# Another order for the beginning of a two-layer cross-attention kernel: the first queries ahead of the keys, the loads regrouped

## The chip, the cores and the metric

The kernel runs on one core of one Trainium2 chip. The metric is the device time of one execution in microseconds. TensorE (PE) multiplies and transposes, VectorE (DVE), ScalarE (ACT) and GpSimd (POOL) work beside it, and SyncE (SP) issues DMAs. ScalarE issues a few as well. Each of the two issues onto a queue of its own, and the two queues share the core's 16 DMA engines.

## The reference

Two cross-attention layers run one after the other over x (16 batches, 256 rows, 160 channels), with a context of 64 tokens by 256 channels for each batch. There are 20 heads of 8 channels.

```python
# layer 0
q = heads(x @ W_q); k_t, v_t = heads(text @ W_k), heads(text @ W_v)     # text = first 60 tokens
probs_t = softmax(q k_t^T * 8**-0.5); text_out = probs_t v_t
k_ip, v_ip = heads(ip @ W_k_ip), heads(ip @ W_v_ip)                     # ip = last 4 tokens
sem = l2norm(probs_t @ text) . l2norm(ip)
probs_ip = softmax(q k_ip^T * 8**-0.5 + 0.5 * sem) * spatial_mask
x = (text_out + probs_ip v_ip) @ W_out + b_out + x
# layer 1: HEADS = 20, TEXT_LEN = 77, so all 64 tokens are text
x = softmax(q k^T * 8**-0.5) v @ Wo.T + bo + x
```

## The kernel before, in words

Work goes by batch: g = 0 to 15 is layer 0, g = 16 to 31 is layer 1. A step t does the core of the attention for batch g = t and the preparation of later batches (t+1: scores for the row maxima; t+3, t+4: queries and keys), and the end of earlier ones (t-1, t-2). Tables written by hand set the order of every engine: `PE_STEP`, `ACT_STEP`, `DVE_STEP`, `POOL_STEP` and `SP_STEP` hold one list for each phase of steps (`PHASES`), and an entry `("q", 3, 0)` in step t means stage q of batch t+3. Stages of batches that do not exist are left out, and those in `ONCE` exist for batch 0 only. Semaphores carry all dependences, so an engine that waits holds everything behind it in its list.

What the beginning does:

- **Warm-up and first loads.** PE does four matmuls on zeros (L521). SP issues the first loads (L428 to L441), ScalarE the two halves of the context `ca` (L725).
- **Keys of layer 0**: PE `project_keys(0, n)` and `project_prompts` (all recorded as L500) for n = 0, later in stage `setup` for n = 1. ACT copies them to `kt` (L731, L738), DVE masks them (L395, L399).
- **Queries of batches 0 and 1** (stage q, for both batches' rows at once, one half of the channels each): PE L500 `ps<-x,wq`.
- **Splits.** Queries and keys are split into three bf16 parts: high (ACT L769, L778), remainder (DVE L845, L409), middle (ACT L773, L782), low (DVE L418, L413). SP then stacks copies of the parts into `qs` and `ks`, six DMAs each (L483 for queries, 160 KB each; L475 for keys, 80 KB each). The score matmuls (stage sc, L572) read only the stacks.
- **Keys of layer 1** (stage `keys1`): PE projects them from `ca` and `wk[1]`. It waits for `rest_in`, a semaphore that counts several loads. ACT copies them to `kt[1]`.
- **The first scores**: sc of batch 0 (L572), whose maxima DVE takes (L889, L898, L901), PE transposes (stage mt, L582), ACT copies (L805) and SP stacks (L488). Then st (L597) makes the scores for the exponentials, exp (L789) and u (L607) follow.
- **Stage vk** multiplies the context by the value weights (L500 `ps<-cw`). It reads `cw`, loaded at L461 (context) and L438 (weights).
- **The rest of x** (batches 4 to 15, 1920 KB) is loaded by SP at L452, the last of the loads that stage `late` holds.

PE order between the warm-up and the main steps, before: keys 0, queries 0 and 1, `setup`, `keys1`, sc of batch 0.

Of the kernel before, what the change touches and what calls it, by code (L numbers as in the profile page):

```python
# [31 lines left out]
N_IP = 4  # L32
# [15 lines left out]
KE = 2  # L48
# [66 lines left out]
def fixed(eng, v):  # L115
# [7 lines left out]

PHASES = (-1, 0, B, B + 2, N_G)
PE_STEP = [
# [14 lines left out]
ACT_STEP = [  # L140
    [("qh", 3, 0), ("kh", 3, 0), ("qm", 3, 0), ("setup", 2, 0), ("km", 3, 0), ("iplen", 2, 0), ("keys1", 2, 0)],
    [("kh", 3, 0), ("km", 3, 0), ("qh", 3, 0), ("mtev", 1, 0), ("qm", 3, 0), ("qh", 4, 0), ("qm", 4, 0)],
    [("exp", 0, 0), ("exp", 0, 1), ("ipe", -2, 0), ("exp", 0, 2), ("exp", 0, 3), ("exp", 0, 4), ("ztev", -2, 0),
# [81 lines left out]
def xattn_kernel(nc, xT, ctxT, ctx0, ctx1, side, WQ, WK, WKIP, WV, WVIP, WO0, WREM, WOP, WO1, BO,  # L225
# [3 lines left out]
    with ExitStack() as stack:  # L229
# [196 lines left out]
        def _(sp):  # L426

            sp.dma_start(wk[0][:, :, :], WK[0]).then_inc(c_in[0], 16)  # L428
            sp.dma_start(wkip[:, :, :], WKIP).then_inc(kv_in[0], 16)
            sp.dma_start(x[:, :, 0:2 * S], xT[:, :, 0:2 * S]).then_inc(x_in[0], 16)  # L430
            sp.dma_start(wq[0][:, :, :], WQ[0]).then_inc(w_in, 16)
            sp.dma_start(cst[:, :], consts).then_inc(w_in, 16)
            sp.dma_start(wvip[:, :, :], WVIP).then_inc(kv_in[1], 16)
            for n in range(2):
                sp.dma_start(ks[n][KR:KM].rearrange("r s a b t -> r (s a b) t"),
                             ones_rows[n].unsqueeze(1).broadcast_to([4, 4 * PAIRS, 128])).then_inc(rows_in, 16)
            for n in range(2):
                sp.dma_start(cw[:, n, :, M2[0] + T:], WV[0]).then_inc(rest_in, 16)  # L438
            sp.dma_start(id16[:, :], ident16).then_inc(rest_in, 16)
            sp.dma_start(x[:, :, 2 * S:4 * S], xT[:, :, 2 * S:4 * S]).then_inc(x_in[1], 16)  # L440
            sp.dma_start(wk[1][:, :, :], WK[1]).then_inc(rest_in, 16)  # L441

            def load_late(a, _):
# [41 lines left out]
            def stack_maxima(a, _):  # L485
# [10 lines left out]
        def _(pe):  # L496
# [25 lines left out]

            pe.wait_ge(c_in[0], 32)
            project_keys(0, 0)
            pe.wait_ge(c_in[1], 16)
            pe.wait_ge(kv_in[0], 16)
            project_prompts(wkip, 6)

            def setup(a, _):
# [9 lines left out]
            def keys1(a, _):  # L539

                pe.wait_ge(setup_sb, 8)
                pe.wait_ge(rest_in, 16 * 4)
                for n in range(2):
                    project_keys(1, n)

            def q(a, _):
                half, lay = a.base % 2, a.layer
                if lay == 0:
                    if a.base == 0:
                        pe.wait_ge(w_in, 32)  # L550
                        pe.wait_ge(x_in[0], 16)
# [164 lines left out]
            run(PE_STEP, {"q": q, "sc": sc, "mt": mt_, "st": st, "u": u, "pv": pv, "quad": quad, "vk": vk, "vw": vw,  # L716
                          "ot": ot, "zt": zt_, "y": y, "setup": setup, "keys1": keys1}, settle)(pe)


        @block.scalar  # L720
        def _(act):
            nc.scalar.preload_act_table_set("natural_log_exp_and_others")
            for n in range(2):
                cols = slice(n * 8 * T, (n + 1) * 8 * T)
                act.dma_start(ca[:, :, cols], ctxT[:, :, cols]).then_inc(c_in[n], 16)  # L725

            def keep_keys(layer, n, first):
# [6 lines left out]

            keep_keys(0, 0, 1)
            act.wait_ge(setup_ps, 4)
            for half in range(2):
                nc.scalar.copy(kt[0][:, half, :, T - N_IP:],  # L738
                               ps[0:HC, 6, half * 64:(half + 1) * 64].rearrange("p (b t) -> p b t", t=N_IP)).then_inc(setup_sb, 1)

# [66 lines left out]
            def ztev(a, _):  # L807
# [9 lines left out]
            run(ACT_STEP, {"otev": otev, "qh": qh, "qm": qm, "kh": kh, "km": km, "exp": exp, "rsq": rsq, "ipe": ipe,  # L817
                           "mtev": mtev, "ztev": ztev, "setup": setup, "iplen": iplen, "keys1": keys1})(act)


        @block.vector
        def _(dve):
# [4 lines left out]
            nc.vector.memset(vpb[:, :, :, 0:IP_ROW], 0.0).then_inc(zeroed, 1)  # L827
            dve.wait_ge(c_in[0], 32)
            dve.wait_ge(c_in[1], 16)
            ipc = ca[:, :, :].rearrange("p k (b t) -> p k b t", t=T)[:, :, :, T - N_IP:]  # L830
            for e in range(KE):
                last = nc.vector.tensor_tensor(ipsq[:, e, :].rearrange("p (b t) -> p b t", t=N_IP), ipc[:, e], ipc[:, e], ALU.mult)
            last.then_inc(sq_made, 1)
            dve.wait_ge(w_in, 32)
            dve.wait_ge(zeroed, 3)
            for n, col in ((0, C_MHH0), (1, C_MHH1)):
                for ring in range(2):
                    nc.vector.tensor_copy(vb[n][:, ring, :, SUM0:SUM0 + 2],
                                          cst[0:M2[n], col:col + 2].unsqueeze(1).broadcast_to([M2[n], PAIRS, 2])).then_inc(vsum, 1)

# [119 lines left out]
            def ysb(a, _):  # L960
# [3 lines left out]
                for mh in range(2):  # L964
# [145 lines left out]
```

## Time and profile before

| what | value |
|---|---|
| median of 3 runs | 513.9 us (513.51 to 517.48) |
| span of the profiled execution | 513.8 us, on core 0, the only one |
| PE busy | 473.6 us, 92% |
| DVE / ACT / POOL busy | 312.9 / 213.8 / 161.8 us |
| mean granted TensorE clock | 0.938 of full |

The profiled execution's own time beside its span: the runs listed are 513.9, 517.48 and 513.51 us, and the span of 513.8 us lies 0.1 us under their median, so the sum of the prediction is made against a span that stands for the median. A digit of the row PEclk is the TensorE clock in a fortieth of the span, in tenths of full speed. A row of the timeline is a run of like instructions of one engine. PE makes two passes for each of the kernel's float32 matmuls, so that `x8` in a row is four matmuls of the program.

### The profile page before, as it was taken

Reading aid. Unit: us, or ns where it says so; the run is one execution under the profiler, and the core shown is the slowest. Engines: PE = TensorE matmul, PEld = TensorE weight load, DVE = VectorE, ACT = ScalarE, POOL = GpSimd, SP = SyncE. Lnnn points to the kernel's source line nnn. Section 1 sums busy time; section 2 is a strip of 40 time slices with the busy share of each in tenths; the row PEclk is TensorE's granted clock in tenths of the full one; section 3 lists DMA queues with packets and bytes.
Section 4 is the critical chain, followed back from the end, with each engine's and each line's share of the span. In section 5 each row is a group of like instructions: output and inputs, shape, how many; then the busy total and the mean of one; then the engine's idle time right before and its main releaser. Section 6 shows DMA issues by size and latency. Waiting matters only on the chain.

```text
span 513.8 us, 10047 instructions
## 1 busy us (share of the span) xinstructions
PE 473.6 (92%) x3100; PEld 255.1 (50%) x3100; DVE 312.9 (61%) x1002; ACT 213.8 (42%) x463; POOL 161.8 (32%) x331
## 2 busy tenths in 40 slices
PE   8968889989999999999999996989898989897996
PEld 4333345545555455554554554555364545454553
DVE  2443686768877787777976776556364445455442
ACT  2413243344444434434354354445354444444361
POOL 0200252453445533555436453422212021221000
PEclk9986998999999999999999999899898597989699
DMA  8995709036073180640905409092728090919011
GB/s 199 130 202 110 95 4 131 18 52 82 18 97 53 31 102 16 83 64 12 120 18 75 64 4 122 8 137 54 115 53 113 23 138 26 139 39 153 2 28 40
DMA packets 33197, 38.15 MB, mean 74 GB/s; under 512 B 4984, under 2 KB 24488, under 8 KB 33000
## 3 DMA queue, kind: packets, MB, share of 16 engines
q1 hardware_dynamic: 32616, 36.63, 47.5%
q10 hardware_dynamic: 544, 1.05, 0.7%
q8 instruction: 20, 0.33, 0.3%
q14 instruction: 17, 0.14, 0.1%
HBM read 10.80 MB, written 2.62 MB: 26 GB/s over the span
## 4 chain that ended last, share of the span: by engine, by line
PE 70%; DMA 16%; SPq 5%; ACT 4%; issue 3%; DVE 1%; ACTq 0%; DVEq 0%
PE ps L500 23%; PE ps L607 14%; DMA qs<-qp 9%; PE ps L634 8%; PE ps L597 8%; PE ps L572 7%; DMA qs<-mt 6%; PE ps L681 4%; SPq L483 4%; PE ps L693 3%; PE ps L649 2%; ACT mt L805 1%; PE ps L582 1%; DMA ca<-in_ctxT 1%; SPq L488 1%
## 5 line engine op out<-in xcount | busy, mean ns | idle before, releaser
L789 ACT ACTIVATE pt<-ps 120x512 f32<-120x512 f32 (+1 forms) x160 | 90.3, 595 | 106.1 <-PE ps L597 105.5
L889 DVE TENSOR_REDUCE mx<-ps 128x8 f32<-128x480 f32 (+3 forms) x192 | 106.3, 577 | 11.6 <-PE ps L572 11.6
L607 PE MATMUL ps<-pt,gram 120*120 120x512 f32 x160 | 81.4, 606 | 0.7 <-ACT pt L789 0.7
L418 POOL TENSOR_TENSOR qp<-qr,qp 80x512 bf16<-80x512 f32 x28 | 32.2, 1151 | 151.9 <-ACT qp L773 151.9
L965 DVE SCALAR_TENSOR_TENSOR x<-ps,bo,x 80x256 f32<-80x256 f32 (+1 forms) x64 | 27.9, 476 | 72.3 <-PE ps L500 72.3
L597 PE MATMUL ps<-qs,ks 100*120 100x256 bf16 (+1 forms) x320 | 63.2, 294 | 8.3 <-DMA qs<-mt 6.0
L500 PE MATMUL ps<-x,wq 80*80 80x512 f32 (+1 forms) x128 | 66.4, 645 | 1.0 <-ACT mt L805 0.9
L572 PEld LDWEIGHTS ps<-ks,qs 96*128 96x128 bf16 x640 | 43.6, 103 | 45.1 <-issue 26.1
L572 PE MATMUL ps<-ks,qs 96*128 96x128 bf16 x640 | 56.9, 231 | 9.2 <-DMA qs<-qp 4.9
L634 PE MATMUL ps<-pt,vb 120*32 120x256 f32 (+1 forms) x640 | 64.3, 410 | 0.0
L500 PE MATMUL ps<-zt,wo 80*80 80x256 f32 (+1 forms) x192 | 55.2, 413 | 8.7 <-ACT zt L815 8.3
L853 DVE TENSOR_TENSOR wt<-ps,pt 120x512 f32<-120x512 f32 x80 | 55.1, 688 | 7.2 <-PE ps L607 3.8
L769 ACT CAST qp<-ps 80x512 bf16<-80x512 f32 x32 | 18.6, 581 | 84.2 <-PE ps L500 59.0
L597 PEld LDWEIGHTS ps<-qs,ks 100*120 100x120 bf16 (+1 forms) x320 | 30.9, 121 | 32.4 <-DMA qs<-mt 13.1
L500 PEld LDWEIGHTS ps<-zt,wo 80*80 80x80 f32 (+1 forms) x192 | 28.5, 159 | 27.5 <-DVE qr L845 9.8
L845 DVE TENSOR_TENSOR qr<-ps,qp 80x512 f32<-80x512 f32 x32 | 21.9, 684 | 29.6 <-ACT qp L769 29.5
L681 PE MATMUL ps<-cst,ots 128*128 128x128 f32 (+1 forms) x192 | 36.7, 286 | 0.8 <-ACT ots L763 0.8
L634 PEld LDWEIGHTS ps<-pt,vb 120*32 120x32 f32 (+1 forms) x640 | 16.5, 111 | 41.9 <-issue 38.4
L761 ACT COPY ots<-ps 128x512 f32<-128x512 f32 x32 | 18.6, 582 | 42.0 <-PE ps L634 41.9
L681 PEld LDWEIGHTS ps<-cst,ots 128*128 128x128 f32 (+1 forms) x192 | 26.0, 148 | 16.9 <-issue 13.0
L864 DVE RECIPROCAL rs<-ps 128x20 f32<-128x20 f32 x64 | 17.7, 277 | 26.4 <-PE ps L681 26.3
L607 PEld LDWEIGHTS ps<-pt,gram 120*120 120x120 f32 x160 | 24.7, 184 | 15.9 <-issue 11.8
(99 smaller groups left out, 605.6 us busy)
## 6 DMA issues: line engine op xcount, KB each, us to landing
qs<-qp SPq DMA_DIRECT2D x96, 160.0 KB, 5.5
ks<-kp SPq DMA_DIRECT2D x96, 80.0 KB, 6.4
cw<-in_ctx SPq DMA_DIRECT2D x16, 184.0 KB, 4.1
out_T<-x SPq DMA_DIRECT2D x16, 160.0 KB, 2.7
cw<-in_ctx SPq DMA_DIRECT2D x16, 128.0 KB, 3.8
x<-in_xT SPq DMA_DIRECT2D x1, 1920.0 KB, 15.2
ca<-in_ctxT ACTq DMA_DIRECT2D x2, 512.0 KB, 7.3
x<-in_xT SPq DMA_DIRECT2D x2, 320.0 KB, 8.9
```

The source lines that it names most:

```text
L418: tt(qp[:, 2, half, :], qr[:, :], qp[:, 1, half, :], ALU.subtract).then_inc(q_l, 1)
L500: last = nc.tensor.matmul(out, l, r, start=(n == 0), stop=(n == len(pairs_) - 1), **kw)
L572: last = nc.tensor.matmul(ps[:, bank, n * 128:(n + 1) * 128], qs[0:KR, slot, pair, c:c + 128], ks[a.layer][0:KR, slot, pair, b2, :], start ...
L597: last = nc.tensor.matmul(ps[0:m, 2 + (a.base + c) % 2, n * S:(n + 1) * S], ks[a.layer][0:KM, slot, pair, b2, 0:m], qs[0:KM, slot, pair, b ...
L607: nc.tensor.matmul(ps[0:M2[0], 4 + (a.base + c) % 2, :], gram[:, a.base % 2, :], pt[0:M2[0], a.base % 2, 2 * c:2 * c + 2, :].rearrange("p ...
L634: last = nc.tensor.matmul(out_of(pair), vb[a.layer][:, a.base % 2, pair, :], pt[0:m, a.base % 2, pair, :], start=(grp != 1), stop=(a.layer ...
L681: last = nc.tensor.transpose(ps[:, bank, grp * 128:grp * 128 + p], ots[0:p, grp, tile * 128:(tile + 1) * 128], cst[0:p, C_ID:C_ID + p])
L789: nc.scalar.activation(pt[0:m, a.base % 2, 2 * c:2 * c + 2, :].rearrange("p a b -> p (a b)"), ps[0:m, 2 + (a.base + c) % 2, :], ACT.Exp, s ...
L845: nc.vector.tensor_tensor(qr[:, :], ps[0:HC, bank_of("q", a, 0), :], qp[:, 0, half, :], ALU.subtract).then_inc(q_r, 1)
L853: nc.vector.tensor_tensor(wt[:, r, 2 * c:2 * c + 2, :].rearrange("p a b -> p (a b)"), ps[0:M2[0], 4 + (a.base + c) % 2, :], pt[0:M2[0], r, ...
L889: nc.vector.tensor_reduce(mx[:, tile, p0:p0 + np_, :], o[:, :, 0:2 * nt].rearrange("p a (h t) -> p a h t", t=nt), AX_X, ALU.max).then_inc( ...
L965: last = nc.vector.scalar_tensor_tensor(x[:, mh, rows], ps[0:HC, bank, mh * S:(mh + 1) * S], bo[:, a.layer, mh:mh + 1], x[:, mh, rows], AL ...
```

## The change

The diff rewrites the first lists of each table and regroups the loads. It computes the same things.

- A phase is added ahead (steps up to -3). In it the queries of batches 0 and 1 are projected, split and stacked, ahead of all keys. The keys of layer 0 become a stage (`keys0`) of the next step, on PE and ACT, and a stage `sums` on DVE holds what DVE did ahead of its first list.
- SP's first loads are x for batches 0 and 1 and `wq[0]`, then `wk[0]`, constants, `wvip`, `ident16`. The loads `WV[0]` (twice), `wk[1]` and the rows of ones become a stage `mid`, issued behind both stacks and the first context.
- The stage `late` is issued one step later, behind the first stacked maxima. Its last load, the rest of x, goes to ScalarE's queue as stage `xrest`, between `iplen` and `keys1`. ScalarE's queue also takes `wkip` and x of batches 2 and 3.
- The semaphores are split to match. In the first main-phase list mt stands ahead of vk on PE, and `mtev` ahead of km and qh on ACT.

```diff
-PHASES = (-1, 0, B, B + 2, N_G)
+PHASES = (-2, -1, 0, B, B + 2, N_G)
 PE_STEP = [
-    [("q", 3, 0), ("setup", 2, 0), ("keys1", 2, 0)],
-    [("sc", 1, 0), ("sc", 1, 1), ("sc", 1, 2), ("sc", 1, 3), ("sc", 1, 4), ("vk", 1, 0), ("mt", 1, 0), ("q", 3, 0),
+    [("q", 3, 0), ("q", 4, 0)],
+    [("keys0", 2, 0), ("setup", 2, 0), ("keys1", 2, 0)],
+    [("sc", 1, 0), ("sc", 1, 1), ("sc", 1, 2), ("sc", 1, 3), ("sc", 1, 4), ("mt", 1, 0), ("vk", 1, 0), ("q", 3, 0),
...
 SP_STEP = [
-    [("qd", 3, 0), ("kd", 3, 0), ("cwd", 2, 0), ("late", 2, 0)],
-    [("mtd", 1, 0), ("cwd", 2, 0), ("qd", 4, 0), ("kd", 3, 0)],
+    [("qd", 4, 0)],
+    [("kd", 2, 0), ("cwd", 2, 0), ("mid", 2, 0)],
+    [("mtd", 1, 0), ("cwd", 2, 0), ("late", 1, 0), ("qd", 4, 0), ("kd", 3, 0)],
...
+            def load_mid(a, _):
+                for n in range(2):
+                    sp.dma_start(cw[:, n, :, M2[0] + T:], WV[0]).then_inc(rest_in, 16)
+                sp.dma_start(wk[1][:, :, :], WK[1]).then_inc(rest_in, 16)
+                for n in range(2):
+                    sp.dma_start(ks[n][KR:KM].rearrange("r s a b t -> r (s a b) t"),
+                                 ones_rows[n].unsqueeze(1).broadcast_to([4, 4 * PAIRS, 128])).then_inc(rows_in, 16)
...
-                sp.dma_start(x[:, :, 4 * S:], xT[:, :, 4 * S:]).then_inc(x_in[2], 16)
...
             def keys1(a, _):
                 pe.wait_ge(setup_sb, 8)
-                pe.wait_ge(rest_in, 16 * 4)
+                pe.wait_ge(rest_in, 16 * 3)
...
+            def xrest(a, _):
+                act.dma_start(x[:, :, 4 * S:], xT[:, :, 4 * S:]).then_inc(x_in[2], 16)
```

The queue of SP between its first loads and the stage `late`, before (names: `kp`, `qp` the split keys and queries, `ks`, `qs` their stacks, `in_WV` and `in_WK` the weights of values and keys):

```order
L440 DMA x<-in_xT 80x2x512
L441 DMA wk<-in_WK 128x320
L475 DMA ks<-kp 16x5x512 [waits k_h]
L475 DMA ks<-kp 16x5x512 x2
L475 DMA ks<-kp 16x5x512 [waits k_m]
L475 DMA ks<-kp 16x5x512
L475 DMA ks<-kp 16x5x512 [waits k_l]
L483 DMA qs<-qp 16x5x1024 [waits q_h]
```

The same place in the change:

```order
L487 DMA qs<-qp 16x5x1024 [waits q_l]
L479 DMA ks<-kp 16x5x512 [waits k_h]
L479 DMA ks<-kp 16x5x512 x2
L479 DMA ks<-kp 16x5x512 [waits k_m]
L479 DMA ks<-kp 16x5x512
L479 DMA ks<-kp 16x5x512 [waits k_l]
L465 DMA cw<-in_ctx 128x2x184
L442 DMA cw<-in_WV 128x2x160 x2
L443 DMA wk<-in_WK 128x320
L445 DMA ks<-in_ones_rows 4x40x128 x2
L492 DMA qs<-mt 4x10x256 [waits mt_sb]
```

`wk[1]` moved from ahead of both stacks to behind them, behind one context load and behind `WV[0]`. The stack of the queries moved ahead of that of the keys.

On PE, from the last matmuls of `setup` to the first `st` (L597), before:

```order
L500 MATMUL ps<-ca,wk 80x512 [waits rest_in,setup_sb]
L500 MATMUL ps<-ca,wk 80x512 x7
L572 MATMUL ps<-ks,qs 128x128 [waits q_r,k_stacked,q_stacked]
...
L500 MATMUL ps<-cw 120x224 [waits setup_sb,rest_in,cw_in0]
L500 MATMUL ps<-cw 120x224
L582 MATMUL ps<-id,mc 40x128 [waits red_done,rest_in,m_lo]
L582 MATMUL ps<-id,mc 40x128
L500 MATMUL ps<-x,wq 80x512 [waits red_done,x_in1]
```

and in the change:

```order
L504 MATMUL ps<-ca,wk 80x512 [waits rest_in,setup_sb]
L504 MATMUL ps<-ca,wk 80x512 x7
L578 MATMUL ps<-ks,qs 128x128 [waits q_r,k_stacked,q_stacked]
...
L588 MATMUL ps<-id,mc 40x128 [waits red_done,id_in,m_lo]
L588 MATMUL ps<-id,mc 40x128
L504 MATMUL ps<-cw 120x224 [waits setup_sb,rest_in,cw_in0]
L504 MATMUL ps<-cw 120x224
L504 MATMUL ps<-x,wq 80x512 [waits red_done,x_in1]
```

`keys1` (the first two rows of each) still stands ahead of the first scores and still waits for `rest_in`, and vk and mt have changed places.

## Rows read from the trace of the kernel before

**Rows 1.** The page: granted clock by slice, and the issue of the rest of x
```profile
PEclk9986998999999999999999999899898597989699
...
x<-in_xT SPq DMA_DIRECT2D x1, 1920.0 KB, 15.2
```

**Rows 2.** Chain that ended last, first 70 us (start us, us, what)
```profile
0.77 5.43 DMA ca<-in_ctxT
...
22.66 9.16 DMA qs<-qp
```

**Rows 3.** Timeline of PE (start us, us, engine, line, operation, count, idle before and releaser)
```profile
6.25 5.40 PE L500 MATMUL ps<-ca,wk 128*80 128x512 f32 x8 [1.01 <-DMA ca<-in_ctxT]
...
15.49 3.60 PE L500 MATMUL ps<-ca,wk 128*80 128x512 f32 x8
...
19.49 0.61 PE L500 MATMUL ps<-ipsq,cst 128*128 128x64 f32 x4
21.32 7.06 PE L500 MATMUL ps<-ca,wk 128*80 128x512 f32 x16 [1.23 <-DMA wk<-in_WK]
31.88 0.62 PE L572 MATMUL ps<-ks,qs 96*128 96x128 bf16 x8 [3.49 <-DMA qs<-qp]
...
34.85 1.79 PE L500 MATMUL ps<-cw 128*120 128x224 f32 x4
36.57 0.40 PE L582 MATMUL ps<-id,mc 128*40 128x128 bf16 x2
36.90 3.70 PE L500 MATMUL ps<-x,wq 80*80 80x512 f32 x4
41.54 3.70 PE L500 MATMUL ps<-x,wq 80*80 80x512 f32 x4 [0.94 <-ACT mt L805]
45.03 0.63 PE L597 MATMUL ps<-qs,ks 100*120 100x256 bf16 x2
...
56.19 1.91 PE L500 MATMUL ps<-x,wq 80*80 80x512 f32 x4
```

**Rows 4.** Timeline of SP's queue
```profile
11.11 0.60 SPq L441 DMA_DIRECT2D wk<-in_WK  x1
15.10 4.33 SPq L475 DMA_DIRECT2D ks<-kp  x6
19.48 3.78 SPq L483 DMA_DIRECT2D qs<-qp  x6
23.30 0.60 SPq L461 DMA_DIRECT2D cw<-in_ctx  x1
```

**Rows 5.** Timeline of ACT
```profile
12.25 0.32 ACT L738 COPY kt<-ps 80x64 f32<-80x64 f32 x2
...
13.98 0.58 ACT L769 CAST qp<-ps 80x512 bf16<-80x512 f32 x1 [1.41 <-PE ps L500]
...
16.96 0.61 ACT L782 CAST kp<-krem 80x512 bf16<-80x512 f32 x1
```

**Rows 6.** Timeline of DVE
```profile
12.67 0.41 DVE L395 TENSOR_TENSOR kmk<-kt,cst 80x240 f32<-80x240 f32 x1 [0.36 <-ACT kt L738]
...
15.72 0.68 DVE L845 TENSOR_TENSOR qr<-ps,qp 80x512 f32<-80x512 f32 x1
```

**Rows 7.** Windows: busy us by engine, then granted clock, DMA share, GB/s
```profile
25.60:26.60 1.00, 1.00 (x4) 0.39 (x3) 0.00 (x0) 0.00 (x0) 0.00 (x0) 1.00 1.08 131
34.00:41.00 7.00, 6.55 (x18) 2.60 (x16) 4.28 (x16) 0.98 (x2) 0.00 (x0) 0.50 0.97 211
44.00:50.00 6.00, 5.05 (x19) 2.81 (x18) 2.38 (x6) 2.48 (x5) 0.00 (x0) 0.72 0.57 106
```

**Rows 8.** DMA queues from 6 to 7 us (q1 is SP's, q10 ScalarE's)
```profile
q1 hardware_dynamic: 91, 0.17, 58.0%
q10 hardware_dynamic: 71, 0.14, 40.1%
```

**Rows 9.** DMA from 34 to 40 us, only the rest of x in flight
```profile
DMA packets 113, 1.30 MB, mean 216 GB/s; under 512 B 2, under 2 KB 8, under 8 KB 8
```

More of the change, by code:

```diff
@@ L140 @@
 ACT_STEP = [
-    [("qh", 3, 0), ("kh", 3, 0), ("qm", 3, 0), ("setup", 2, 0), ("km", 3, 0), ("iplen", 2, 0), ("keys1", 2, 0)],
-    [("kh", 3, 0), ("km", 3, 0), ("qh", 3, 0), ("mtev", 1, 0), ("qm", 3, 0), ("qh", 4, 0), ("qm", 4, 0)],
[3 rows of a table added]
     [("exp", 0, 0), ("exp", 0, 1), ("ipe", -2, 0), ("exp", 0, 2), ("exp", 0, 3), ("exp", 0, 4), ("ztev", -2, 0),
@@ L164 @@
 POOL_STEP = [
+    [],
     [("iplen", 2, 0)],
@@ L186 @@
 BY_BLOCK = ("kh", "km", "kmask", "kr", "kl", "kd")
-ONCE = ("late", "setup", "iplen", "keys1")
-FIRST_STEP, LAST_STEP = -4, N_G + 1
+ONCE = ("mid", "late", "xrest", "keys0", "setup", "iplen", "keys1", "sums")
+FIRST_STEP, LAST_STEP = -3, N_G + 1
 LOOPS = {4: 2, B + 2: 2}
@@ L286, in xattn_kernel @@
         ps = stack.enter_context(nc.psum_tensor("ps", [128, 8, 512], F32))
-        w_in, rest_in, late_in = sem("w_in"), sem("rest_in"), sem("late_in")
+        w_in, wq_in, id_in, rest_in, late_in = (sem(n) for n in ("w_in", "wq_in", "id_in", "rest_in", "late_in"))
         c_in, kv_in = [sem(f"c_in{n}") for n in range(2)], [sem(f"kv_in{n}") for n in range(2)]
@@ L426, in _ @@
         def _(sp):
+            sp.dma_start(x[:, :, 0:2 * S], xT[:, :, 0:2 * S]).then_inc(x_in[0], 16)
+            sp.dma_start(wq[0][:, :, :], WQ[0]).then_inc(wq_in, 16)
             sp.dma_start(wk[0][:, :, :], WK[0]).then_inc(c_in[0], 16)
-            sp.dma_start(wkip[:, :, :], WKIP).then_inc(kv_in[0], 16)
-            sp.dma_start(x[:, :, 0:2 * S], xT[:, :, 0:2 * S]).then_inc(x_in[0], 16)
-            sp.dma_start(wq[0][:, :, :], WQ[0]).then_inc(w_in, 16)
             sp.dma_start(cst[:, :], consts).then_inc(w_in, 16)
             sp.dma_start(wvip[:, :, :], WVIP).then_inc(kv_in[1], 16)
[L434 to L441, printed above, removed]
+            sp.dma_start(id16[:, :], ident16).then_inc(id_in, 16)
+            def load_mid(a, _):
[5 more added lines that the diff above has]
+                                 ones_rows[n].unsqueeze(1).broadcast_to([4, 4 * PAIRS, 128])).then_inc(rows_in, 16)
             def load_late(a, _):
@@ L488, in stack_maxima @@
                 sp.dma_start(qs[KR:KM, slot, :, b2 * S:(b2 + 1) * S], mt[:, b2, :]).then_inc(m_stacked[b2], 16)
-            run(SP_STEP, {"late": load_late, "cwd": load_context, "outd": store, "kd": stack_keys, "qd": stack_queries,
+            run(SP_STEP, {"mid": load_mid, "late": load_late, "cwd": load_context, "outd": store, "kd": stack_keys, "qd": stack_queries,
                           "mtd": stack_maxima})(sp)
@@ L521, in _, with keys0 @@
                 nc.tensor.matmul(ps[:, 0, 0:S], wt[:, 0, 0, 0:128], wt[:, 0, 1, :], start=True, stop=True)
[L523 to L527, printed above, removed]
+            def keys0(a, _):
+                pe.wait_ge(c_in[0], 32)
+                project_keys(0, 0)
+                pe.wait_ge(c_in[1], 16)
+                pe.wait_ge(kv_in[0], 16)
+                project_prompts(wkip, 6)
             def setup(a, _):
@@ L716, in _ @@
             run(PE_STEP, {"q": q, "sc": sc, "mt": mt_, "st": st, "u": u, "pv": pv, "quad": quad, "vk": vk, "vw": vw,
-                          "ot": ot, "zt": zt_, "y": y, "setup": setup, "keys1": keys1}, settle)(pe)
+                          "ot": ot, "zt": zt_, "y": y, "keys0": keys0, "setup": setup, "keys1": keys1}, settle)(pe)
         @block.scalar
@@ L733, in keep_keys, with keys0 @@
                                    ).then_inc(setup_sb, 1)
[L735 to L739, printed above, removed]
+            def keys0(a, _):
+                keep_keys(0, 0, 1)
+                act.wait_ge(setup_ps, 4)
+                for half in range(2):
+                    nc.scalar.copy(kt[0][:, half, :, T - N_IP:],
+                                   ps[0:HC, 6, half * 64:(half + 1) * 64].rearrange("p (b t) -> p b t", t=N_IP)
+                                   ).then_inc(setup_sb, 1)
+            def xrest(a, _):
+                act.dma_start(x[:, :, 4 * S:], xT[:, :, 4 * S:]).then_inc(x_in[2], 16)
             def setup(a, _):
@@ L817, in _ @@
             run(ACT_STEP, {"otev": otev, "qh": qh, "qm": qm, "kh": kh, "km": km, "exp": exp, "rsq": rsq, "ipe": ipe,
-                           "mtev": mtev, "ztev": ztev, "setup": setup, "iplen": iplen, "keys1": keys1})(act)
+                           "mtev": mtev, "ztev": ztev, "keys0": keys0, "xrest": xrest, "setup": setup, "iplen": iplen, "keys1": keys1})(act)
         @block.vector
@@ L827, in _, with sums @@
             nc.vector.memset(vpb[:, :, :, 0:IP_ROW], 0.0).then_inc(zeroed, 1)
[L828 to L839, printed above, removed]
+            def sums(a, _):
+                dve.wait_ge(c_in[0], 32)
+                dve.wait_ge(c_in[1], 16)
+                ipc = ca[:, :, :].rearrange("p k (b t) -> p k b t", t=T)[:, :, :, T - N_IP:]
+                for e in range(KE):
+                    last = nc.vector.tensor_tensor(ipsq[:, e, :].rearrange("p (b t) -> p b t", t=N_IP), ipc[:, e], ipc[:, e], ALU.mult)
+                last.then_inc(sq_made, 1)
+                dve.wait_ge(w_in, 16)
+                dve.wait_ge(zeroed, 3)
+                for n, col in ((0, C_MHH0), (1, C_MHH1)):
+                    for ring in range(2):
+                        nc.vector.tensor_copy(vb[n][:, ring, :, SUM0:SUM0 + 2],
+                                              cst[0:M2[n], col:col + 2].unsqueeze(1).broadcast_to([M2[n], PAIRS, 2])).then_inc(vsum, 1)
             def qr_(a, _):
@@ L967, in ysb @@
                 last.then_inc(y_sb, 1)
-            run(DVE_STEP, {**splits(dve, nc.vector.tensor_tensor), "qr": qr_, "w": w, "on": on, "red": red, "neg": neg, "ipa": ipa, "ipm": ipm, "ipr": ipr, "vprep": vprep,
+            run(DVE_STEP, {**splits(dve, nc.vector.tensor_tensor), "qr": qr_, "sums": sums, "w": w, "on": on, "red": red, "neg": neg, "ipa": ipa, "ipm": ipm, "ipr": ipr, "vprep": vprep,
                            "wz": wz_, "ysb": ysb})(dve)
```

19 lines of the change are left out of this document (11 added, 8 removed), and 3 rows, old and new, of the table ACT_STEP.

## The prediction

> **What bounds the kernel now.** I read the page's busy shares first. PE is busy for 92% of the span, so the main steps belong to PE, and only the beginning of the kernel has stretches in which PE waits. The diff touches the beginning alone. I then read the chain that ended last for the first 70 us. It opens with 5.43 us of the context's load, and its one long piece after that is the landing of the stacked queries, 9.16 us [rows 2]. PE's timeline shows what this costs. The keys of layer 1 (16 passes, 7.06 us) end at 28.38 us, PE stands for 3.49 us, and the first scores begin at 31.88. The granted clock is then 0.50 from 34 to 41 us and 0.72 on average from 44 to 50, so that q of 4 passes takes 3.70 us instead of 1.91 and the first st waits until 45.03 [rows 3, 7]. The first st is my milestone, because from it on both kernels issue the same work. The whole question is when it starts in the change.
>
> **First queries.** They now come first. They need 420 KB of x and `wq[0]` on one queue beside the context's 512 KB on the other, which landed 6.20 us after the start (0.77 + 5.43) [rows 2], so I start them at 6.5. The first eight passes behind the warm-up took 5.40 us and later ones 3.60 [rows 3]. Queries end at 11.9. The splits add one high cast, one remainder, one middle cast and one low subtraction, about 0.6 us each [rows 5, 6]: the low part is made at 14.4. SP's first query DMA goes at about 12.6 and six take 3.78 us [rows 4], so the last is issued near 16.5. This removes the 9.16 us landing from the chain: the query stacks, 960 KB at 131 GB/s [rows 7], are down by about 22 us, where they landed at 31.83. Taken alone this would take out PE's 3.49 us of waiting.
>
> **First keys.** They come 5.6 us later than they did. Keys of layer 0 on PE run from 11.9 to 15.5 (3.60) and the prompts take 0.7 more, 16.2. Two small copies (0.32), the masks (0.9 for the four, from the 0.41 of the large ones), then high cast, remainder, middle cast and low subtraction (0.62, 0.68, 0.61, 0.68) [rows 5, 6] put the low keys at 20.2. SP's key DMAs go from about 18.5 to 22.3, where they ended at 19.43 [rows 4]. Their data stand behind the queries' in the queue: 480 KB at 131 GB/s from 22 on is 3.7 us, so about 25.5. That is still ahead of the 31.88 at which scores began, and by itself costs nothing.
>
> **The load that `keys1` needs.** Here the change adds a wait. `keys1` stands on PE ahead of the first scores and waits for `WV[0]` twice and `wk[1]`. `wk[1]` was issued at 11.11, and PE started on it at 21.32 after a wait of only 1.23 us [rows 3, 4]. It is now behind both stacks, one context load and two `WV[0]`. Four issues of 0.60 us from 22.3 on end at 24.7. PE ends `setup` at about 20.9 (16.2 plus the 4.6 from 15.49 to 20.10 [rows 3]), so it idles. The data before and with `wk[1]`, 664 KB, start behind the key stacks at about 25.2.
>
> They do not travel alone. ScalarE issues the rest of x, 1920 KB, after `iplen`, at about 22.5 by my timeline. Before, it stood in the same queue behind everything and took 15.2 us to land while nobody needed it [rows 1]. Now it is in the other queue and shares the engines. How the engines share is the disputed term, and its bounds are these.
> - Lower: the loads pass as if x were absent: 664 KB at about 250 GB/s is 2.6 us, plus 0.7 to land: 28.5.
> - Middle: equal bytes. At 230 GB/s in total 1330 KB take 5.8 us: 31.7.
> - Upper: x first. x alone runs at 216 GB/s, 9.1 us from 24.3 [rows 9], then the rest: 36.7.
>
> The row nearest to it is the one in which both queues had work: 91 packets of SP's against 71 of ScalarE's, 0.17 against 0.14 MB [rows 8]. It reads as turns by packet. The packets of x's rest are of 12 KB (1.30 MB in 113 packets, eight of them small [rows 9]), those of `WV[0]` 640 bytes, so turns by packet give x nearly everything. I take 34.5, nearer to the upper end. **`keys1` starts at 34.5**, 13.2 us later.
>
> **How long `keys1` takes.** It has 16 passes: 7.06 us at full clock, 14.8 at half, from 3.70 for four [rows 3]. Before it PE will have been idle for about 13 us. In the present trace an idle stretch of 3.5 us with sparse work behind it took the clock down, and it came back only near 48 us [rows 7]. The first eight passes after the idle start cost 1.8 us extra, and here are twice as many. I take 10.0 us, nearer to 7.06 + 1.8 because `keys1` runs without gaps. The first scores start at 44.5 instead of 31.88: **+12.6 us**.
>
> The Trainium skill (TensorE: Matmul & The Clock Gate, section The HAM clock gate) says the default state is throttled and activity releases it. By it 7.06 for `keys1` is excluded after such a wait, which agrees with the row of the first eight passes. By the row's lowest reading the sum would be 1.1 us less than mine.
>
> **From the first scores to the first st.** Before, 13.15 us [rows 3]. The scores are paced by DVE's maxima, 4.69 us to mt, and stay so. vk (1.79 at half clock) used to fill PE's time ahead of mt and now stands behind it, so it adds its own time; in exchange `mtev` no longer waits behind qh, which removes the 0.94 us wait. At full clock mt, vk and two q take 0.2 + 0.9 + 1.9 + 1.9, less overlap, and st starts 9.4 us after the scores; at half it would be 13.9. After `keys1` the clock should be up, so 9.4: **-3.7 us**. The stretch from 45 to 48 us also ran at half clock with 2.3 us of it on PE: **-1.2 us**. The stack of the maxima is issued some 5.3 us after the scores and lands well before st.
>
> **What costs nothing.** The late loads are first read by the vw of batch 0, a whole step behind the first st; without that step of cover their landing, 6 to 8 us by my estimate from the 9.16 of the stacks, would show on PE. The rows of ones are needed at st only, more than 10 us after their issue. The second context load is issued after the first stacked maxima, close to the vk of batch 1 right behind st: up to 1 us if it is late, which I leave in the range. SP's, ScalarE's and POOL's other instructions are the same in number.
>
> **Sum.** +12.6 - 3.7 - 1.2 = +7.7 us on a span of 513.8, which is 0.1 under the median: 521.5 us.
>
> **The rivals.**
> - *The keys' load comes early* (0.22). If sharing is by bytes, `keys1` starts at 31.7 and the first scores at 41.7: +9.8 - 4.9, 518.7 us. At the lower bound of 28.5, with `keys1` at its full-clock 7.06 us, scores start at 35.6: +3.7 - 4.9 is 512.6 us. This is the case that is not slower: it decides for the change once `wk[1]` lands before about 30 us. What speaks for it is that SP's loads are issued at much the same time as x's; against it stand the packet sizes.
> - *x goes first and PE stays cold* (0.16). `keys1` starts at 36.7 or later, and with the clock low until its end takes 14.8: scores at 51.5, st 13.9 behind: +20 us, 534. With 10.0 and a fast clock it is 523.7. The long low stretch from 34 to 48 us speaks for it, the gaps in that stretch against.
> - *A faster kernel by more than 1%* (0.07). The queries' landing is gone and the wait for `wk[1]` would have to vanish too, which its issue at 24.7 excludes. What is left is the later course: the clock row shows several dips in the second half [rows 1], and a shifted start can move them. Three dips less would be 508.
> - The forecast itself has 0.55, from 519 to 524.
>
> The Trainium skill (DMA: Bandwidth & Descriptors, section Queues, rings and completion order) says that each DMA engine serves the queues in turn, a whole packet of several descriptors at a time. By it x's large pieces would pass in groups and SP's loads would wait for nearly all of x, 523.7 us by the sum above; the row of two queues agrees with turns, and none here shows turns with pieces this unequal.
>
> **How the numbers follow.** A measurement of this kernel tells about 1%, 5.1 us, from no change. Slower by more than that, over 519.0, holds nearly all of the forecast, the cold case and a part of the first rival: 0.66. Within 1% lies most of the first rival and the forecast's lower edge: 0.27. Faster is 0.07. The range is 514 to 528: it leaves out the 534 end, the best case of the first rival and the faster case, some 0.2 together.
>
> **What would show it.** In the profile after: PE's q ahead of all keys from about 6.5 us; the last query stack issued by 17 and SP's last key stack near 22; `wk[1]` issued near 25; PE idle from 21 until 31 to 37 us with `wk[1]` as releaser, and a low clock in `keys1`; the first L578 scores at 41 to 47, the first st at 51 to 56, and from there the same distance to the end as before (468.7 us) within 2 us. I am wrong if `wk[1]` lands before 30 us, or if the clock stays up through the idle stretch, or if steps behind the first st change by more than the shift.

## The result, and the profile after

The change is slower. Its four runs have a median of 535.34 us (526.4 to 540.15), the kernel before 514.58 beside it. The ratio is 1.031 with a 95% interval of 1.023 to 1.039. The forecast of 521.5 us had the sign right and half the size, and the time lies outside its range of 514 to 528. The profiled execution has a span of 530.1 us, 16.3 more than before. Executions of one unchanged kernel differ by 10 us and more: in 35 of them the kernel before took from 508.24 us, at a mean granted clock of 0.954, to 521.96, at 0.916. The ratio leaves out executions over 1.5% above the fastest of their kernel and the median does not, so the two do not give the same difference. Times are therefore read beside places in the profile.

First the page of the changed kernel: its span, PE's busy time, the granted clock by slice, and the issue of the rest of x.

```profile
span 530.1 us, 10047 instructions
PE 477.2 (90%) x3100; PEld 256.7 (48%) x3100; DVE 313.4 (59%) x1002; ACT 214.4 (40%) x463; POOL 162.3 (31%) x331
...
PEclk8858599899999999999999999899979597989699
...
x<-in_xT ACTq DMA_DIRECT2D x1, 1920.0 KB, 12.3
```

PE is busy 3.6 us longer and the span grew by 16.3, so most of the loss is PE standing still. Two of the first five slices have a clock of 5 tenths, where before none of them was under 6 [rows 1].

PE's timeline of the change, with the rows that answer to [rows 3] (start, duration, idle before and releaser):

```profile
7.41 5.45 PE L504 MATMUL ps<-x,wq 80*80 80x512 f32 x8 [2.17 <-DMA wq<-in_WQ]
12.65 5.24 PE L504 MATMUL ps<-ca,wk 128*80 128x512 f32 x8
...
22.30 0.61 PE L504 MATMUL ps<-ipsq,cst 128*128 128x64 f32 x4
38.85 9.26 PE L504 MATMUL ps<-ca,wk 128*80 128x512 f32 x16 [15.94 <-DMA wk<-in_WK]
47.94 0.61 PE L578 MATMUL ps<-ks,qs 96*128 96x128 bf16 x8
...
52.48 0.29 PE L588 MATMUL ps<-id,mc 128*40 128x128 bf16 x2 [1.58 <-DVE mc L916]
52.70 1.09 PE L504 MATMUL ps<-cw 128*120 128x224 f32 x4
53.59 7.03 PE L504 MATMUL ps<-x,wq 80*80 80x512 f32 x8
60.41 0.63 PE L603 MATMUL ps<-qs,ks 100*120 100x256 bf16 x2
```

PE stands for 15.94 us with `wk[1]` as the releaser; before, the wait at this place was 1.23 [rows 3]. No wait for the stacked queries is left. The first st starts at 60.41 instead of 45.03, 15.4 us later. From there to the end it is 469.7 us against 468.8, so in this pair of traces the beginning holds 15.4 of the 16.3 us. That the rest is so small is partly luck: in a second trace of the change the same stretch took 474.8.

Beside it SP's queue, and the one row of ScalarE's queue that matters, as in [rows 4]:

```profile
13.51 3.84 SPq L487 DMA_DIRECT2D qs<-qp  x6
20.49 3.75 SPq L479 DMA_DIRECT2D ks<-kp  x6
24.29 0.61 SPq L465 DMA_DIRECT2D cw<-in_ctx  x1
24.94 1.81 SPq L442 DMA_DIRECT2D cw<-in_WV  x2
26.79 0.63 SPq L443 DMA_DIRECT2D wk<-in_WK  x1
```
```profile
24.14 0.65 ACTq L752 DMA_DIRECT2D x<-in_xT  x1
```

The issues are about where the prediction had them, two microseconds late. What was not is the landing. `wk[1]` took 11.93 us to land, in the chain that ended last:

```profile
26.79 11.93 DMA wk<-in_WK
```

The two queues from 26 to 30 us and from 30 to 33 us, packets and MB (to be held beside [rows 8]):

```profile
q10 hardware_dynamic: 65, 0.80, 88.7%
q1 hardware_dynamic: 1, 0.00, 0.1%
```
```profile
q10 hardware_dynamic: 54, 0.66, 99.7%
q1 hardware_dynamic: 54, 0.04, 6.8%
```

At first x passed nearly alone: 65 of its packets to one of SP's, although SP had issued the context load at 24.29. Then 54 packets of x passed and 54 of SP's. In bytes that is 0.66 MB against 0.04, sixteen to one. **Where the two queues took turns, they took them by piece, and a 12 KB piece counted as much as a 736-byte one.** Both parts stand in the second trace of the change as well: 55 to none from 28 to 31 us, then 53 to 51 from 32 to 35. From 30 to 35 us the engines moved 220 GB/s, nearly all of it the load that nobody needed yet (1.01 of 1.10 MB), and SP's queue had 0.50 MB left to move from 35 to 37.

The granted clock in three stretches (the first number behind POOL's column is the clock): 

```profile
39.00:44.00 5.00, 5.00 (x7) 1.54 (x8) 0.00 (x0) 0.58 (x1) 0.00 (x0) 0.57 0.09 4
44.00:54.00 10.00, 7.26 (x37) 3.58 (x36) 4.76 (x17) 3.15 (x6) 0.00 (x0) 0.98 0.00 0
54.00:60.00 6.00, 6.00 (x8) 1.74 (x7) 2.49 (x7) 1.20 (x2) 0.00 (x0) 0.50 0.45 117
```

The clock came back during `keys1`, as forecast, and fell a second time behind the thinly filled scores, so that the two q ran at half clock (7.03 us for eight passes). It was still 0.50 from 60 to 67 us, behind the first st.

### The profile page after: what moved, and what is told of

Read it like the earlier page. It is cut to its first block, busy times and chain, and to the rows that moved or that the text cites. A ratio compares the mean times of both kernels' runs of the same rounds, so it can differ in the third digit from the quotient of the medians.

```text
span 530.1 us, 10047 instructions
## 1 busy us (share of the span) xinstructions
PE 477.2 (90%) x3100; PEld 256.7 (48%) x3100; DVE 313.4 (59%) x1002; ACT 214.4 (40%) x463; POOL 162.3 (31%) x331
## 4 chain that ended last, share of the span: by engine, by line
PE 69%; DMA 18%; SPq 5%; ACT 3%; issue 3%; DVE 2%; ACTq 0%; DVEq 0%
PE ps L504 23%; PE ps L613 14%; PE ps L603 8%; PE ps L640 7%; DMA qs<-mt 7%; PE ps L578 7%; DMA qs<-qp 7%; PE ps L686 4%; SPq L487 3%; PE ps L698 3%; DMA wk<-in_WK 2%; PE ps L655 2%; ACT mt L818 1%; PE ps L588 1%; DMA wq<-in_WQ 1%
## 5 line engine op out<-in xcount | busy, mean ns | idle before, releaser
L504 PE MATMUL ps<-x,wq 80*80 80x512 f32 (+1 forms) x128 | 67.8, 659 | 2.3 <-DMA wq<-in_WQ 2.2
L504 PEld LDWEIGHTS ps<-zt,wo 80*80 80x80 f32 (+1 forms) x192 | 28.5, 159 | 27.4 <-DVE qr L860 9.7
```

Source lines behind the costliest of these rows:

```text
L504: last = nc.tensor.matmul(out, l, r, start=(n == 0), stop=(n == len(pairs_) - 1), **kw)
```

## The experiments

Each profile is read at the same four places, from rows of PE's timeline. "To the end" is the span less the start of the first st.

| kernel | `keys1` starts, takes | scores | first st | to the end | median us (beside before) |
|---|---|---|---|---|---|
| before | 21.32, 7.06 | 31.88 | 45.03 | 468.8 | 514.58 |
| before, again | 20.53, 7.09 | 31.42 | 44.93 | 468.4 | 516.25 (515.61) |
| change | 38.85, 9.26 | 47.94 | 60.41 | 469.7 | 535.34 (514.58) |
| change, again | 39.99, 8.74 | 48.56 | 59.30 | 474.8 | 531.58 (516.12) |
| e1 change, x behind on SP | 30.65, 10.07 | 40.55 | 49.60 | 477.8 | 525.51 (515.16) |
| e2 change, wk early | 24.52, 7.09 | 31.45 | 47.35 | 479.2 | 517.1 (515.16) |
| e3 change, PE kept busy | 41.20, 8.79 | 49.83 | 61.86 | 470.6 | 534.77 (515.16) |
| e4 before, wk late | 30.82, 9.45 | 40.11 | 50.35 | 465.3 | 520.84 (515.16) |
| e5 before, x on ScalarE's queue | 20.85, 7.09 | 37.60 | 51.10 | 462.4 | 517.14 (516.12) |
| e6 change, both repairs | 24.86, 7.09 | 31.79 | 43.55 | 464.5 | 514.62 (516.12) |
| e8 e6, `keys1` behind scores | 34.28, 9.90 | 28.95 | 48.22 | 461.5 | 518.13 (516.12) |
| e11 e6, scores filled up | 24.32, 7.09 | 31.25 | 42.10 | 468.0 | 513.92 (515.61) |
| e12 e6, old mt order | 23.34, 7.09 | 30.27 | 41.02 | 479.1 | 513.87 (515.61) |
| e13 before, new mt order | 23.60, 7.09 | 30.53 | 42.84 | 470.6 | 516.9 (515.61) |

The instructions behind the first st are the same in all of them, and the last stretch still ranges from 461.5 to 479.2 us. It goes with the clock. In e5 (462.4) the granted clock over that stretch is 0.95, in e2 (479.2) it is 0.91:

```profile
51.10:513.40 462.30, 432.14 (x2999) 237.97 (x2997) 297.72 (x955) 201.24 (x437) 159.07 (x318) 0.95 0.45 66
```
```profile
47.30:526.50 479.20, 451.33 (x2999) 245.95 (x2997) 297.39 (x955) 201.63 (x437) 158.60 (x318) 0.91 0.44 64
```

So the start of the first st tells edits of the beginning apart, and a single span does not. The ratios below are to the kernel before, by its executions at about the same time.

**e1: the rest of x behind `wk[1]`, on SP's queue.** My theory was that turns by piece starve SP's loads; the rival was that the position behind the stacks is enough.

```diff
-("iplen", 2, 0), ("xrest", 2, 0), ("keys1", 2, 0)]
+("iplen", 2, 0), ("keys1", 2, 0)]
 def load_mid(a, _):
...
+    sp.dma_start(x[:, :, 4 * S:], xT[:, :, 4 * S:]).then_inc(x_in[2], 16)
```

> The change, with the rest of x taken off ScalarE's queue and issued by SP as the last load of mid, behind wk[1] and the rows of ones. Theory A (two queues take turns by piece, so the 12 KB pieces of x starve SP's small ones): the key stacks are down at about 25.5 us, 664 KB follow at 250 GB/s, keys1 starts at 29 us instead of 38.85, with the clock still low in part of it, and the run is 8 to 10 us shorter than the change, 521 to 524. Rival B (position behind the stacks alone makes wk[1] late, the other queue does not matter): keys1 starts within 2 us of 38.85 and the time stays at 530 or more.

```profile
30.65 10.07 PE L505 MATMUL ps<-ca,wk 128*80 128x512 f32 x16 [6.97 <-DMA wk<-in_WK]
...
49.60 0.38 PE L604 MATMUL ps<-qs,ks 100*120 100x256 bf16 x2
```

`keys1` starts 8.2 us earlier and the first st 10.8, with the same loads in the same place on SP. `wk[1]` landed 3.50 us after its issue instead of 11.93. The rival falls. That x stood in the other queue is the cause; e1 does not tell turns by piece from the stretch in which x passed alone. The median of 525.51 is 10 us under the change's, but its four executions lie from 517.33 to 529.23 and the comparison has no interval, so the start of `keys1` is the evidence. PE still waits 6.97 us, the part that belongs to the position.

**e2: `WV[0]` and `wk[1]` with the first loads, x still on ScalarE's queue.**

```diff
     sp.dma_start(id16[:, :], ident16).then_inc(id_in, 16)
+    for n in range(2):
+        sp.dma_start(cw[:, n, :, M2[0] + T:], WV[0]).then_inc(rest_in, 16)
+    sp.dma_start(wk[1][:, :, :], WK[1]).then_inc(rest_in, 16)
```

> The change, with WV[0] twice and wk[1] issued with SP's first loads, ahead of the query stack; the rest of x stays on ScalarE's queue. Both theories: keys1 starts when setup ends, about 23.5 us, at full clock, 7.1 us. Theory A and the clock theory: scores start at 30.6, the first st at about 41 (it waits for the rows of ones, still behind x), 60.41 before: 19 us less, 509 to 512. If the change's cost lies elsewhere (the clock after a late start, the order of mt and vk), it stays above 518.

```profile
24.52 7.09 PE L504 MATMUL ps<-ca,wk 128*80 128x512 f32 x16 [0.46 <-ACT inv L758]
...
38.89 1.85 PE L504 MATMUL ps<-cw 128*120 128x224 f32 x4 [2.61 <-DMA cw<-in_ctx]
40.53 7.04 PE L504 MATMUL ps<-x,wq 80*80 80x512 f32 x8
47.35 0.63 PE L603 MATMUL ps<-qs,ks 100*120 100x256 bf16 x2
```

`keys1` runs at once and at full clock, and the scores start at 31.45. But my 41 us for the first st was wrong: it came at 47.35. The queue of x found the next victim, the context load of vk (2.61 us), and the clock was 0.50 from 37 us on, so the two q took 7.04. The time, 517.1, is 5 us over what I expected, and the ratio is 1.020 (1.011 to 1.030).

**e3: PE kept busy through the wait.**

```diff
 def keys1(a, _):
     pe.wait_ge(setup_sb, 8)
+    for _ in range(34):
+        nc.tensor.matmul(ps[:, 2, 0:S], wt[:, 0, 0, 0:128], wt[:, 0, 1, :], start=True, stop=True)
     pe.wait_ge(rest_in, 16 * 3)
```

> The change, with 34 matmuls on zeros (68 passes of 256 columns) on PE between setup and keys1, so that PE does not stand idle while wk[1] is on its way. No load and no wait differs. The start of keys1 stays near 39 us. If the idle stretch's clock is what made keys1 9.26 us long and put the two q at half clock (7.03 us for eight passes against 3.6), keys1 takes 7.1, the first st comes about 5.5 us earlier than 60.41 and the run takes 524 to 526. If the clock there does not depend on the idle stretch, nothing changes.

```profile
23.28 14.94 PE L549 MATMUL ps<-wt 120*128 120x256 f32 x68 [0.46 <-ACT inv L760]
41.20 8.79 PE L504 MATMUL ps<-ca,wk 128*80 128x512 f32 x16 [2.98 <-DMA wk<-in_WK]
...
55.44 6.63 PE L504 MATMUL ps<-x,wq 80*80 80x512 f32 x8
```

This expectation failed. The fillers ran at full clock for 14.94 us, and what was left, 2.98 us of idle time, was followed by a low stretch in `keys1` (8.79). The q behind the scores ran at half clock all the same, 0.50 from 56 to 61.8 us. The long idle stretch is therefore not what slowed the q here, and the first st at 61.86 gained nothing. The ratio is 1.054 (1.040 to 1.068). My claim of 5.5 us for the clock of the wait falls.

**e4: the order alone, in the kernel before.** `WV[0]` and `wk[1]` are issued behind both stacks and the first context load. Everything stays on SP's queue.

```diff
-    for n in range(2):
-        sp.dma_start(cw[:, n, :, M2[0] + T:], WV[0]).then_inc(rest_in, 16)
...
-    sp.dma_start(wk[1][:, :, :], WK[1]).then_inc(rest_in, 16)
     def load_late(a, _):
+        for n in range(2):
+            sp.dma_start(cw[:, n, :, M2[0] + T:], WV[0]).then_inc(rest_in, 16)
+        sp.dma_start(wk[1][:, :, :], WK[1]).then_inc(rest_in, 16)
```

> The kernel before, with WV[0] twice and wk[1] issued behind both stacks and the first context load (ahead of the late loads and the rest of x, all on SP). It has the position of the change without the second queue. Theory A: the stacks are down near 31 us, 664 KB behind them take 3 us, keys1 starts at about 34.5 instead of 21.3 and takes 9.3, scores at 44 instead of 31.88, 8 to 12 us slower than before, 522 to 526. Were the position harmless, keys1 would start before 26 and the time stay within 2 us of before.

```profile
30.82 9.45 PE L500 MATMUL ps<-ca,wk 128*80 128x512 f32 x16 [11.72 <-DMA wk<-in_WK]
40.11 0.61 PE L572 MATMUL ps<-ks,qs 96*128 96x128 bf16 x8
...
50.35 0.43 PE L597 MATMUL ps<-qs,ks 100*120 100x256 bf16 x2 [0.66 <-DMA qs<-mt]
```

The position costs 9.5 us at `keys1` and 8.2 at the scores. Only 5.3 remain at the first st, since the clock in this trace is up for the q behind it (1.94 us for four passes against 3.70). The ratio to before is 1.030 (1.013 to 1.048), the median 520.84. `keys1` started 3.7 us earlier than I expected and the time is 1 us under the lower end of my 522 to 526.

**e5: the second queue alone, in the kernel before.**

```diff
-                sp.dma_start(x[:, :, 4 * S:], xT[:, :, 4 * S:]).then_inc(x_in[2], 16)
...
+            def xrest(a, _):
+                act.dma_start(x[:, :, 4 * S:], xT[:, :, 4 * S:]).then_inc(x_in[2], 16)
```

> The kernel before, with one thing of the change alone: the rest of x issued on ScalarE's queue, between iplen and keys1 (at about 22 us). Theory A (turns by piece): wk[1] has landed by then, so keys1 starts at 21.3 as before, but the query stacks (2 KB pieces, 60 a us) now take turns with 12 KB pieces, one for one, and land at about 36 to 39 instead of 31.83; scores and the first st come 4 to 7 us later, 517 to 522. Rival (the engines share by bytes or SP's queue comes first): stacks land within 2 us of 31.83 and the time is that of before.

```profile
20.85 7.09 PE L499 MATMUL ps<-ca,wk 128*80 128x512 f32 x16 [0.77 <-ACT inv L747]
37.60 1.03 PE L571 MATMUL ps<-ks,qs 96*128 96x128 bf16 x8 [9.65 <-DMA qs<-qp]
...
51.10 0.64 PE L596 MATMUL ps<-qs,ks 100*120 100x256 bf16 x2
```

and in its chain of waits

```profile
22.65 14.90 DMA qs<-qp
```

where the kernel before had 9.16 [rows 2]. With the other queue loaded, the query stacks landed 5.7 us later, and the first st 6.1 later. The mechanism hits whatever stands in the other queue: the query stacks here, `wk[1]` in the change, vk's context in e2. The packets show the same two parts: 31 of x to 2 of SP's from 27 to 29 us, then 49 to 49 from 31 to 34. The time is only 1.010 times before (1.001 to 1.020), and its profile has the second-shortest stretch to the end.

**e6: both repairs on the change.**

> The change with both repairs: WV[0] and wk[1] among SP's first loads, and the rest of x on SP behind the rows of ones. keys1 at 24.5, scores at 31.5, no wait of vk for its context load (2.61 us with x on ScalarE's queue), the first st at 40.5 if the clock stays up through the scores, at 44 if it falls again. 505 to 511, equal to or 1% faster than the kernel before.

```profile
24.86 7.09 PE L505 MATMUL ps<-ca,wk 128*80 128x512 f32 x16 [0.46 <-ACT inv L759]
31.79 0.61 PE L579 MATMUL ps<-ks,qs 96*128 96x128 bf16 x8
...
37.40 6.36 PE L505 MATMUL ps<-x,wq 80*80 80x512 f32 x8
43.55 0.63 PE L604 MATMUL ps<-qs,ks 100*120 100x256 bf16 x2
```

Its edit is that of e1 with that of e2. No wait for a load or a stack is left between `keys1` and st, and all of the change's loss is gone: 0.998 times before (0.993 to 1.003), 514.62 us. It does not gain either. The scores start at 31.79 us, where the kernel before had them at 31.88, for another reason: the first queries start 7 to 8 us after the beginning, and PE's work up to the end of `keys1` fills the time that the stacks' landing took before. Four microseconds over my 505 to 511.

**e8: e6 with `keys1` behind the first scores.** ScalarE's list moves in the same way.

```diff
-    [("keys0", 2, 0), ("setup", 2, 0), ("keys1", 2, 0)],
-     ("sc", 1, 4), ("mt", 1, 0), ("vk", 1, 0),
+    [("keys0", 2, 0), ("setup", 2, 0)],
+     ("sc", 1, 4), ("mt", 1, 0), ("keys1", 1, 0), ("vk", 1, 0),
```

> As the last, and keys1 moved behind the first scores and mt on PE (behind mtev and km on ScalarE), so that its 7.1 us fill the stretch in which PE waited for maxima. Scores start when the key stacks land, at about 28 us, st of batch 0 behind keys1, vk and two q at 42 to 44: PE's sum is the same and PE now waits for the stacks instead. 506 to 512, the same as the last within 2 us. If the clock falls in the wait for the stacks, 3 to 5 us worse.

```profile
28.95 1.01 PE L579 MATMUL ps<-ks,qs 96*128 96x128 bf16 x8 [5.04 <-issue]
...
34.28 9.90 PE L505 MATMUL ps<-ca,wk 128*80 128x512 f32 x16
44.02 0.92 PE L505 MATMUL ps<-cw 128*120 128x224 f32 x4
```

The last sentence of the expectation is what happened: PE waited 5.04 us ahead of the first scores (the row names no releaser; these matmuls read the stacks, the last of which SP had issued by 25.2), the clock was 0.50 from 27 to 34 us, `keys1` took 9.90, and the first st came at 48.22, 4.7 us behind e6. The ratio is 1.005 (1.000 to 1.011).

**e9 and e10: the two kernels again.**

> The change once more, unchanged. keys1 at 38 to 40 us behind a wait for wk[1] in every profile, if the cause is the order of the loads; the distance from the first st to the end may differ by several us with the clock's low stretches, as it did between profiles so far (465.3 to 479.2 us).

> The kernel before once more, unchanged, for a second trace: scores at 31 to 33 us behind the query stack, first st at 44 to 46, and the distance from there to the end anywhere between 462 and 479 us, longer where the clock was low for longer, if the course of the clock differs between executions of one kernel.

```profile
39.99 8.74 PE L504 MATMUL ps<-ca,wk 128*80 128x512 f32 x16 [16.27 <-DMA wk<-in_WK]
```
```profile
44.93 0.63 PE L597 MATMUL ps<-qs,ks 100*120 100x256 bf16 x2
```

Both came out as expected. The wait for `wk[1]` is 16.27 us in the second trace of the change, and its ratio 1.034 (1.025 to 1.042). Between the two traces of one kernel the first st moved by 0.1 and 1.1 us, which is the measure for the differences above.

**e11: the scores filled up.** On e6, eleven short matmuls on zeros where PE waits for the maxima.

```diff
+def busy(a, n):
+    for _ in range(n):
+        nc.tensor.matmul(ps[:, 6, 0:128], wt[:, 0, 0, 0:128], wt[:, 0, 1, 0:128], start=True, stop=True)
-    ("sc", 1, 1), ("sc", 1, 2), ("sc", 1, 3), ("sc", 1, 4), ("mt", 1, 0)
+    ("sc", 1, 1), ("busy", 1, 2), ("sc", 1, 2), ("busy", 1, 1), ("sc", 1, 3), ("busy", 1, 1), ("sc", 1, 4), ("busy", 1, 7), ("mt", 1, 0)
```

> The kernel with both repairs, and 11 short matmuls on zeros (128 columns) put between the groups of the first scores and ahead of mt, where PE waits for DVE's maxima. If the thinly used scores take the clock down (low from 38.4 us in the last profile of this kernel), the clock now stays up, the two q take 3.6 us instead of 6.36, the first st starts at 40.5 to 41.5 instead of 43.55, and the run gains 3 to 6 us: 507 to 511 at the median, 1% under the kernel before. If these passes do not hold it, st stays at 43.5 and the median near 514.

```profile
36.86 3.60 PE L505 MATMUL ps<-x,wq 80*80 80x512 f32 x8
42.10 0.43 PE L608 MATMUL ps<-qs,ks 100*120 100x256 bf16 x2 [1.65 <-DMA qs<-mt]
```

The q took 3.60 us instead of 6.36, and 1.65 us of these 2.8 went into a new wait: the stacked maxima stand in SP's queue behind the rest of x. The ratio is 0.992 (0.982 to 1.003), so no gain is shown.

**e12 and e13: the place of mt alone.** e12 is e6 with vk ahead of mt and `mtev` behind qh again; e13 is the kernel before with the new places.

> The kernel with both repairs, with mt behind vk and mtev behind km and qh again, as in the kernel before. The scores start at 31.8 as without it. q of the second half waits for mtev behind the first (0.94 us), vk fills PE's wait for the maxima (1.58 falls to 0.7 or less): the first st within 1.5 us of 43.55, a little later if the clock is up, since a stacked maximum lands just ahead of st. Time within 1% of it.

> The kernel before with only mt and mtev moved ahead, as the change has them. Scores at 31.9, the first st between 44 and 45.5 against 45.03, time within 1% of before. If st comes 2 us or more earlier, this edit alone is what the repaired kernel gains over the kernel before.

```profile
37.90 1.94 PE L505 MATMUL ps<-x,wq 80*80 80x512 f32 x4 [0.94 <-ACT mt L819]
41.02 0.43 PE L604 MATMUL ps<-qs,ks 100*120 100x256 bf16 x2 [1.18 <-DMA qs<-mt]
```

Both expectations missed the first st. The rows are of e12, where it came 2.5 us ahead of e6's 43.55, in part because the scores started 1.5 us earlier. In e12 the clock was up for the q without any filler (1.94 for four passes), so e11 does not show that its fillers did it. In e13 the scores started at 30.53 without a wait for the stacks and st at 42.84, 2.2 us ahead of the kernel before; 1.4 of these were there at the scores, and the stretch behind them, 12.31 us against 13.15, is 0.8 shorter.

What the order is worth with the clock up can be read only roughly. From the scores to the first st e12 took 10.75 us, and e1, with the new order and an equally high clock, 9.05. But 1.18 us of e12 are the wait for the stacked maxima, issued behind the rest of x, and e11 has the new order and 1.65 us of the same wait in 10.85. Without that wait it is 9.57 with the old order and 9.05 and 9.20 with the new one: some 0.4 to 0.5 us. In the totals no gain shows: e12 has 0.995 (0.990 to 1.001), and e13 1.007 (1.002 to 1.011), a little slower than before.

## Why the prediction had the sign and missed the size

Two terms failed: **"`keys1` starts at 34.5"**, and within it the price of sharing, and **the clock behind `keys1`** ("the clock should be up", -3.7 and -1.2). The span missed the forecast by 8.6 us. The scores started 3.5 us later than forecast, the stretch from them to the first st took 3.0 more, and what lies behind it 2.1 more. With the start of `keys1` alone put right, at 38.85, the sum would have been 525.9 us, inside the range, so the price of sharing alone does not explain the miss.

- *The wait itself* was right: PE idle from 22.9 us with `wk[1]` as releaser, and nothing else between. e1, e4 and e5 show its two parts separately. The position behind the stacks is worth 9.5 us at `keys1` (e4 against before). The second queue is worth 8.2 more (change against e1). e6 takes both away, and the loss is gone.
- *The sharing.* I had weighed turns by packet against equal bytes and chosen 34.5 between them, though the only row with both queues loaded [rows 8] spoke for turns. The price was higher than that of turns: 65 pieces of x to one of SP's, and then 54 to 54. The Trainium skill's rule (DMA: Bandwidth & Descriptors, section Queues, rings and completion order), which I had set down as a rival, names the same direction. The trace agrees with it in that a group of x's pieces passed first, and differs from it behind that group, where single pieces alternated and not packets of several descriptors.
- *The upper bound* of 36.7, x first and SP's loads behind it, was nearest to what happened. It was too low by 2.2 us, since everything ahead had slipped. x of batches 0 and 1 and `wq[0]` landed at 7.4, not 6.5; the first keys took 5.24 us at a low clock, not 3.60; SP's issue of the three loads ended at 27.4, not 24.7, and that of x was at 24.14, not 22.5.
- *`keys1`* took 9.26, not 10.0. The scores came 16.1 us later instead of 12.6.
- *From scores to st* I took 9.4 us, a high clock. It was 12.47, since the clock fell a second time. So the term was -0.7 instead of -3.7, and the -1.2 behind st was +0.9, with the clock still at 0.50 there. The sum of the three, +16.1 - 0.7 + 0.9, is the measured 16.3. This part varies between executions: in the second trace of the change the clock came back sooner, the q took 4.74 us and the stretch 10.74.
- *The rival "x goes first and PE stays cold"* comes nearest: 523.7 to 534. Its first half happened, and not its second in that form: the clock was back in `keys1` and gone again in the q. In e3, filling the wait did not help.
- *What cost nothing* did: the stacked queries, the late loads, the rows of ones and the maxima show no wait ahead of the first st in the change's profile.
- *The range* left out what executions of one kernel differ by. From the first st on it was 461.5 to 479.2 us here.

What stays open is what decides in one execution whether the clock falls behind the scores. It fell in e2, e3, e6, e13 and both traces of the change, not in e1, e4 and e12, though the same passes stand ahead of it in e6 as in the change and e1. It also stays open why a first group of x's pieces passed nearly alone before the turns began. No version is shown to be faster than the kernel before; e6, e8, e11 and e12 equal it within their intervals.

## What to carry to other kernels

Before a large load is moved to a second queue, look at what is in flight in the first at that moment: with pieces of 12 KB against pieces under 1 KB the first queue is all but stopped until the large load ends, so such a load belongs behind the small ones that are needed sooner, in the same queue. What is issued behind it then waits in turn, as the stacked maxima did in e11 and e12 (1.65 and 1.18 us). When a stage is moved to the back of an issue list, go through every count its semaphore stands for; here the load that a 7 us block of PE needed was listed with loads that could wait. And ahead of a front made earlier, ask whether the front was the bound: the queries' stacks landed in time, and nothing came of it, because PE's own work up to the first scores was as long.

## What the runs showed of the hardware that was not expected

- With two queues at work on the same DMA engines, the load of 12 KB pieces first passed nearly alone (65 pieces to one in 4 us), and then single pieces alternated: 54 of 12 KB to 54 of 736 bytes in 3 us, 0.66 to 0.04 MB.
- The granted clock differs between executions of one kernel (0.916 to 0.954 in 35 of the kernel before). The last 2,999 matmul passes, the same in all kernels here, took 462.3 us at 0.95 in e5 and 479.2 at 0.91 in e2.
- Passes on zeros held the clock up for 14.94 us, and 3 us of idle time behind them were followed by a low stretch (0.57 from 42 to 46 us in e3).
